# Gathers in a four-layer graph network: what GpSimd waits for before it issues the next one

## What is computed

```python
# layer 0, twice: attention over the incoming edges of a node, 4 heads of 32
kj = k[src] + e
vj = v[src] + e
alpha = einsum('ehc,ehc->eh', q[dst], kj) / sqrt(C)
p = exp(alpha - segment_max(alpha, dst)[dst])
w = p / segment_sum(p, dst)[dst]
out = segment_sum(vj * w, dst) + x @ Ws + bs
# layer 1: an MLP of each node over [x, sum of edge_attr]
# layer 2: relation attention, whose score of an edge has a part from its source
score = s_node[src, etype] + d_node[dst, etype] + s_rel[etype]
# layer 3, twice: a weighted sum of rows of x[src] @ W[edge_type]
out = segment_sum((xj @ W[r]) * edge_weight, dst) + x @ root + bias
```

## Time and profile before

| | us |
|---|---|
| median of 3 runs | 8819.53 |
| lowest, highest | 8816.77, 8831.27 |
| the profiled execution's own time | 8871.76 |
| its span, first to last instruction | 8869.8 |
| busy: PE, DVE, ACT, POOL | 3145.1, 3340.3, 1098.0, 4141.1 |
| mean granted clock of PE | 0.61 of full speed |

### The profile page before, as it was taken

How to read it: one execution, slowest core, us unless ns; L and a number is a source line. 1 busy time by engine, 2 the same in 40 slices (tenths; PEclk the granted TensorE clock), 3 DMA queues, 4 the chain that set the end, 5 groups by cost and what they waited for, 6 DMA issues and landing times. The chain is left out here.

```text
span 8869.8 us, 97993 instructions
## 1 busy us (share of the span) xinstructions
PE 3145.1 (35%) x21507; PEld 2692.6 (30%) x21508; DVE 3340.3 (38%) x8392; ACT 1098.0 (12%) x2790; POOL 4141.1 (47%) x4444
## 2 busy tenths in 40 slices
PE   3455555544444544434420000133222224222222
PEld 1454554542444444423320000122222223222222
DVE  6454444455444444455210002982222222222223
ACT  1222222211222222231000000010000001000000
POOL 1444445432555555512555554124555553555554
PEclk7677776776665555566555555556665567655655
DMA  3444444432333333311210000002111112111111
GB/s 117 120 124 119 125 125 117 126 116 89 90 91 92 92 91 88 92 51 49 71 33 0 0 0 4 0 21 71 38 39 39 39 39 84 38 39 39 39 38 45
DMA packets 396582, 583.18 MB, mean 66 GB/s; under 512 B 112981, under 2 KB 272994, under 8 KB 395874
## 3 DMA queue, kind: packets, MB, share of 16 engines
q0 software_dynamic: 160752, 337.32, 14.0%
q1 hardware_dynamic: 235634, 244.06, 8.5%
HBM read 522.34 MB, written 58.72 MB: 66 GB/s over the span
## 5 line engine op out<-in xcount | busy, mean ns | idle before, releaser
L617 POOL DMA_INDIRECT kv<-kv_table,idx x1760 | 1690.1, 960 | 1769.5 <-DMA kv<-kv_table,idx 1206.1
L1822 POOL DMA_INDIRECT rows_in<-rel_table,idx x1568 | 1489.1, 950 | 1156.0 <-DMA rows_in<-rel_table,idx 585.3
L1116 PE MATMUL ps_s<-rows_in,onehot 128*128 x3520 | 717.5, 387 | 2000.7 <-SPq L1835 1755.0
L1116 PEld LDWEIGHTS ps_s<-rows_in,onehot 128*128 128x128 f32 x3520 | 668.1, 291 | 2050.1 <-issue 2047.8
L1543 POOL DMA_INDIRECT from_src<-score_table,idx x784 | 752.3, 960 | 558.8 <-DMA from_src<-score_table,idx 309.7
L1143 DVE TENSOR_TENSOR acc<-acc,ps_s 128x128 f32 x880 | 250.6, 285 | 1812.0 <-PE ps_s L1116 1779.9
L749 PE MATMUL ps_q<-qsplit,st 128*128 x5280 | 557.9, 290 | 1055.7 <-DVE kv L812 917.6
L735 PE MATMUL ps_s<-pv,lent 128*128 128x136 f32 x3520 | 820.9, 386 | 108.1 <-DVE acc L794 96.4
L812 DVE TENSOR_TENSOR kv<-ps_q,kv 128x528 f32<-128x528 f32 x440 | 303.2, 706 | 1435.2 <-DMA kv<-kv_table,idx 1236.1
L749 PEld LDWEIGHTS ps_q<-qsplit,st 128*128 128x128 bf16 x5280 | 504.1, 133 | 1111.6 <-issue 1097.1
L735 PEld LDWEIGHTS ps_s<-pv,lent 128*128 128x128 f32 x3520 | 706.7, 280 | 149.2 <-DVE acc L794 125.5
(11 more groups left out here) (296 smaller groups left out, 3982.0 us busy)
## 6 DMA issues: line engine op xcount, KB each, us to landing
dl_row<-dloc_slots SPq DMA_DIRECT2D x132, 640.0 KB
eb<-in_edge_attr SPq DMA_DIRECT2D x440, 128.0 KB
kv<-kv_table,idx POOLq DMA_INDIRECT x1760
rows_in<-rel_table,idx POOLq DMA_INDIRECT x1568
flags<-flag_rows SPq DMA_DIRECT2D x88, 168.0 KB
rel_table<-y_out SPq DMA_DIRECT2D x14, 1024.0 KB, 4.3
from_src<-score_table,idx POOLq DMA_INDIRECT x784
rel_table<-y_out SPq DMA_DIRECT2D x14, 768.0 KB, 3.6
```

Of the source, the lines that this page charges most:

```text
L617: pool.indirect_dma_start(kv4[:, k, s, 0:KVW], None, kv_table, bass.IndirectOffsetOnAxis(ap=idx[:, k * CB + s:k * CB + s + 1], axis=0))\
L1116: last_mm = pe.matmul(to, one(n, j), ring_rows(places[m], j), start=(j == 0), stop=(j == 1))
L1822: pool.indirect_dma_start(rows3[:, t, :], None, table, bass.IndirectOffsetOnAxis(ap=idx[:, t:t + 1], axis=0)).then_inc(landed[lane].sem, 16)
```

## The change

The lanes are gone. `indirect_dma_start` gets a second semaphore, `engine_sem=described.sem`, which goes up by one when GpSimd has written the gather's descriptors. Before each gather POOL waits for that count, that is for the end of the issuing work of the gather directly ahead, and no longer for any landing. Landings are counted in a semaphore for each half of the buffer (`gathered[k]`) or each part, and the readers wait on that one. SP fetches the indices of chunk c+2 when the gathers of chunk c have landed, where it waited until DVE had summed chunk c. The order of the instructions on the engines is the same, but that in POOL's loops a register instruction that computes the value to wait for stands ahead of each gather, where it stood ahead of each two. All else is untouched.

```diff
-LANES = 2
@@ conv_stream
-                landed = [signal(f"cs_landed{n}") for n in range(LANES)]
-                TURNS = CB // LANES
+                described = signal("cs_described")
...
                             for s in range(CB):
-                                turn, lane = divmod(s, LANES)
-                                if again or c * CB + s >= LANES:
-                                    pool.wait_ge(landed[lane].sem, landed[lane].at(c * (16 * TURNS) + 16 * turn))
+                                if again or c * CB + s > 0:
+                                    pool.wait_ge(described.sem, described.at(c * CB + s))
                                     pool.sem_inc(issuing.sem, 1)
                                 pool.indirect_dma_start(
                                     kv4[:, k, s, 0:KVW], None, kv_table,
-                                    bass.IndirectOffsetOnAxis(ap=idx[:, k * CB + s:k * CB + s + 1], axis=0))\
-                                    .then_inc(landed[lane].sem, 16)
+                                    bass.IndirectOffsetOnAxis(ap=idx[:, k * CB + s:k * CB + s + 1], axis=0),
+                                    engine_sem=described.sem)\
+                                    .then_inc(gathered[k].sem, 16)
...
                             if later(c, 2):
-                                sp.wait_ge(summed.sem, summed.at(c + 1))
+                                sp.wait_ge(gathered[k].sem, gathered[k].at((j + 1) * (16 * CB)))
                                 sp.sem_inc(issuing.sem, 1)
                                 fetch_idx(c + 2, k)
...
-                            for sig in landed:
-                                dve.wait_ge(sig.sem, sig.at((c + 1) * (16 * TURNS)))
+                            dve.wait_ge(gathered[k].sem, gathered[k].at((j + 1) * (16 * CB)))
@@ relation_scores
-                                    turn, lane = divmod(s, LANES)
-                                    if again or s >= LANES:
-                                        pool.wait_ge(landed[lane].sem, landed[lane].at(i * (32 * TURNS) + 16 * turn))
+                                    if again or s > 0:
+                                        pool.wait_ge(described.sem, described.at(i * (2 * CT) + s))
                                         pool.sem_inc(issuing.sem, 1)
...
-                                for sig in landed:
-                                    act_e.wait_ge(sig.sem, sig.at(i * (32 * TURNS) + (k + 1) * (16 * TURNS)))
+                                act_e.wait_ge(gathered[k].sem, gathered[k].at((i + 1) * (16 * CT)))
@@ rgcn_sums
-                                    turn, lane = divmod(t, LANES)
-                                    if again or t >= LANES:
-                                        pool.wait_ge(landed[lane].sem, landed[lane].at(i * (16 * TURNS) + 16 * turn))
+                                    if again or t > 0:
+                                        pool.wait_ge(described.sem, described.at(i * (2 * RP) + t))
                                         pool.sem_inc(issuing.sem, 1)
...
-                                for sig in landed:
-                                    sp.wait_ge(sig.sem, sig.at(i * (16 * TURNS) + (c + 1) * (16 * OF_PART)))
+                                sp.wait_ge(gathered[c].sem, gathered[c].at((i + 1) * (16 * 2 * RC)))
```

More of the change, by code:

```diff
@@ L565, in conv_stream @@
                 issuing = signal("issuing")
-                idx_in, e_in = ((signal("cs_" + n + "0"), signal("cs_" + n + "1")) for n in ("idx_in", "e_in"))
-                landed = [signal(f"cs_landed{n}") for n in range(LANES)]
-                TURNS = CB // LANES
+                idx_in, gathered, e_in = ((signal("cs_" + n + "0"), signal("cs_" + n + "1")) for n in ("idx_in", "gathered", "e_in"))
+                described = signal("cs_described")
                 kv4 = kv[:, :].rearrange("p (k s c) -> p k s c", k=2, s=CB)
@@ L894, in conv_stream @@
                           cs_stepped=CP * NCH, cs_added=CP * NCH, cs_rescaled=2 * (NCH - 1), cs_chained=LINKS * NCH,
-                          cs_cleared=1, cs_idx_in0=16 * NPAIR, cs_idx_in1=16 * NPAIR,
-                          **{f"cs_landed{n}": 16 * TURNS * NCH for n in range(LANES)})
+                          cs_cleared=1, cs_idx_in0=16 * NPAIR, cs_idx_in1=16 * NPAIR, cs_gathered0=16 * CB * NPAIR,
+                          cs_gathered1=16 * CB * NPAIR, cs_described=CB * NCH)
                 if with_edges:
@@ L1516, in relation_scores @@
                 st_made = (signal("rs_st0"), signal("rs_st1"))
-                issuing = signal("issuing")
+                issuing, described = signal("issuing"), signal("rs_described")
                 kept = (signal("rs_kept0"), signal("rs_kept1"))
-                dl_in, summed = ((signal(n + "0"), signal(n + "1")) for n in ("rs_dl_in", "rs_summed"))
-                landed = [signal(f"rs_landed{n}") for n in range(LANES)]
-                TURNS = CT // LANES
+                gathered, dl_in, summed = ((signal(n + "0"), signal(n + "1")) for n in ("rs_gathered", "rs_dl_in", "rs_summed"))
                 st4 = st[:, :].rearrange("p (k s e) -> p k s e", k=2, s=CB)
@@ L1544, in once @@
                                         from_src[:, s:s + 1], None, flat_scores,
-                                        bass.IndirectOffsetOnAxis(ap=idx[:, s:s + 1], axis=0)).then_inc(landed[lane].sem, 16)
+                                        bass.IndirectOffsetOnAxis(ap=idx[:, s:s + 1], axis=0),
+                                        engine_sem=described.sem).then_inc(gathered[k].sem, 16)
                         once(0, False)
@@ L1797, in rgcn_sums @@
                 idx_ready, issuing, pairs_in, stepped = (signal(n) for n in ("rg_idx", "issuing", "rg_pairs_in", "rg_stepped"))
-                landed = [signal(f"rg_landed{n}") for n in range(LANES)]
-                TURNS = 2 * RP // LANES
-                OF_PART = 2 * RC // LANES
+                gathered = [signal(f"rg_gathered{c}") for c in range(RP // RC)]
+                described = signal("rg_described")
                 rows3 = rows_in[:, :].rearrange("p (t c) -> p t c", c=D)
@@ L1823, in once_round @@
                                         rows3[:, t, :], None, table,
-                                        bass.IndirectOffsetOnAxis(ap=idx[:, t:t + 1], axis=0)).then_inc(landed[lane].sem, 16)
+                                        bass.IndirectOffsetOnAxis(ap=idx[:, t:t + 1], axis=0),
+                                        engine_sem=described.sem).then_inc(gathered[c].sem, 16)
                         once_round(0, False)
@@ L1837, in rgcn_sums @@
                           (lambda place, j: rows_in[:, bass.ds(place * (2 * D) + j * D, D)], pairs_in, stepped, place_of))
-                stage_end(rg_idx=LAPS * (RP // RC), rg_pairs_in=LAPS * RP, rg_stepped=NCH * CP,
-                          **{f"rg_landed{n}": 16 * TURNS * LAPS for n in range(LANES)})
+                stage_end(rg_idx=LAPS * (RP // RC), rg_pairs_in=LAPS * RP, rg_described=2 * RP * LAPS, rg_stepped=NCH * CP,
+                          **{f"rg_gathered{c}": 16 * 2 * RC * LAPS for c in range(RP // RC)})
         tables()
```

## The result

The changed kernel takes 8897.9 us (median of 4 runs, 8893.34 to 8898.57), the kernel before 8820.78 beside it: a ratio of 1.0084, 95% interval [1.0067, 1.0102]. It is slower, by 0.8%, where faster was forecast. Its profiled execution took 8897.98 us with a span of 8896.0; against the profiled execution of before (8871.76) that is only 26 us more. The 8871.76 lies outside the four timed runs of the kernel before (8816.77 to 8831.27).

The account below looks back on a forecast made before the run. The prediction took POOL's issue of indirect gathers to bound the kernel. Stage changes of -36 us and -4 for index copies made -40, so 8819.5 - 40 = 8780 us, range 8690 to 9030.

Parts of the forecast that it names:

- What bounds the kernel: In all five gather stages, 83% of the span, POOL's issue of gathers from start to start sets the time.
- Step (a): Before every gather: the wait for the predecessor's descriptors makes each pause 0.82 us, within bounds of 0.30 and 1.14.
- tail: Rival, all 4112 gathers: the engine's semaphore comes after the bar's end; 0.05 us later gives 8985 us; chance 0.12.
- rows 7: Profile rows of POOL with index copy, wait for that copy, then gather: pauses of 0.84, 0.83 and 0.81 us.
- Step (b): Pauses by stage: convolutions -145 and -105 us, scores +84, aggregations +65 each, sum -36; index copies -4; total -40.
- I put the difference on the median: Baseline: profiled execution 52 us over the runs' median; the -40 was applied to 8819.5, giving 8780 us.
- Step (c): Convolutions: the gain passes through, chunk periods falling 3.3 and 2.4 us, with some 10 us of DVE's cover left.
- Step (d): Elsewhere (SP's index fetches, readers' single counts, POOL's register instruction): extra losses and gains are nothing.
- Step (e): DMA queues: with one start each 1.77 us about two gathers are in flight, as before, so little changes.
- The waits' name: In the profile, POOL's waits before gathers would be put down to POOL itself and not to a DMA.
- Landing waits go and nothing comes in: Rival: POOL's 2101.1 us of landing idle vanishes, leaving 6718 us, or about 6660 by 0.30 us pauses; chance 0.05.
- convolutions without gain: Rival, both convolutions: transfers set the pace, so the -250 stays away and +214 comes, 9030 us; chance 0.08.

Follow-up runs that it names:

- group 2: Changed kernel with no wait between gathers: 9687.84 us; changed kernel with each gather waiting for descriptors of the gather two ahead: 9566.29 us.
- threes: Changed kernel, with POOL waiting for descriptors only before every third gather in all three loops: 8482.16 us, ratio 0.9621.
- pairs: Changed kernel, with POOL waiting for descriptors only before every second gather in all three loops: 7923.47 us, ratio 0.8927.

## Why the prediction was wrong

*What bounds the kernel* held: where the start-to-start time fell and the others were not held back, the stage gained it in full.

*Step (a)* held in mechanism: hardly a pause under 0.8, no tail, a median of 0.81 where I took 0.82. What failed is "every pause becomes that of rows 7". 77 gathers have a pause of over 1.0 us that is no index copy's doing (18 in the convolutions, 7 in the scores, 52 in the aggregations), like the 1.66 at 6215.94, and behind the 123 index copies within the stages it is mostly 0.96 to 0.98 us and not 0.83. Of the 77, 64 stand at fixed places: 3.25 us at every hundredth gather of a convolution, 3.52 at every 112th of the scores, 1.66 (three times 1.98) at every 32nd of an aggregation. They are no landings: at 6215.94 the wait had been met at 6214.32. The 77 cost about 96 us over 0.81, the index copies about 20, and all other pauses, being 0.81 and not 0.82, give back about 51. In the kernel before, the trace shows such a pause at some of these places and not at others, so its waits for landings covered them in part; nothing covers them now. *Step (b)* thereby: pauses 7 and 9 us over the forecast in the convolutions, 10 in the scores, 17 and 17 in the aggregations, together 60; the index copies gained nothing in the changed kernel (idle 16.6 and 16.1 us where 7.8 and 16.6 stood before): +8 and not -4; busy time 9 less. -40 + 60 + 12 - 9 = +23, for a difference of +26 between the two profiled executions. This alone turned the sign: on one chip the change costs 23 us where the sum said -40.

*"I put the difference on the median"* is the second failure, and made a loss of 0.3% one of 0.8%. The profiled execution of before stood 52 us over its median, and I took this for something the change would carry along. The changed kernel has no such gap: profiled 8897.98, median 8897.9. 66 us of the sum and 52 of the baseline are the 118 between 8780 and 8898. The repeated runs speak against the profiler as the cause (8869.1 profiled, 8870.03 timed on one chip) and show that the kernel before differs from one set of runs to the next, each on another chip. It waits for single landings, the changed kernel doesn't, and that one agrees within 5 us in the two sets that timed it. That landings differ by chip is therefore my reading, and shown by no run; why the profiled execution of before stood 52 us apart stays open.

*Step (c)* held: the convolutions are 139 and 100 us shorter for a forecast of 145 and 105, and DVE kept its wait for rows (1005.5 us). *Step (d)* held: the five stages account for 23 of the 26 us. *Step (e)* held: in the convolutions a gather takes some 2.8 us from its start to its landing, with a start each 1.75 us, so one or two are in flight.

*The waits' name* was foretold wrongly: the profile says DMA, not POOL.

*Rivals.* There is no tail: the wait is met 0.034 us after the bar's end, and the pauses are 0.81. The convolutions did gain. "Landing waits go and nothing comes in" got 0.05 and a time of 6660 to 6718 for the case that pauses fall to 0.30. The runs of group 2 made those pauses and took 9688: the price of 0.30, used as bound of (a) as well, had a cost on other engines that no row of before shows. There the Trainium skill, page "DMA: Bandwidth & Descriptors", section "Anatomy of one DMA — SWDGE (gpsimd) path", says that most of such a DMA's fixed time is completion latency. This case's trace agrees (rows land 1.8 us after the bar, median of the convolutions), but the forecast that the rival drew from it fails: 8898 us without waiting for completions, and a larger loss when the pauses are gone.

*The chances*: with 0.01 us of pause worth 41 us, and a median on another footing than the trace, 0.53 for faster was too much for a sum of -40. That 8898 lies within the stated range of 8690 to 9030 bears out nothing: the range was wide for a tail and for convolutions without gain, and neither came.

## What to carry to other kernels

A stream of indirect gathers is paced by what stands between two of them: here 0.30 us with nothing, 0.81 for a wait on the one ahead, about 1.2 for a landing in the convolutions. In this kernel a wait on descriptors before every second or third gather was best. Try the grouping by stage: threes won in the scores and aggregations and lost in the convolutions, where the other queues have more to do. Don't take the shortest pause for the best one without a look at what the other engines do meanwhile. And before a difference of profiles is put on a median, see whether the profiled execution and the timed ones of the kernel before agree.

## What the hardware showed unexpectedly

- With gathers issued at 1.25 us from start to start, the queues of TensorE and SP are held back: the `ps_d` matmuls of a stage take 1406 instead of 391 us, ten DMA issues 21.33 instead of 5.65. At 1.43 and 1.38 us the convolutions still lose hundreds of us. At about 1.5 us little of it is seen (305.2 us of idle time at `ps_d` with pairs against 217.4), or none (215.1 in the kernel with the multiply).
- With a multiply of 0.54 us on POOL between gathers the kernel is 1540 us faster than with a copy of 0.20 us in its place (7736.93 and 9277.11, each on its own chip, where the kernel before takes 8798.5 and 8905.1).
- From POOL's wait on its own work to the next gather 0.81 us pass, behind an independent instruction 0.16.
- A wait for a gather's descriptors is met 0.034 us after its bar ends; the rest of the 0.81 us lies between the met wait and the engine's start.
- The kernel before differs by 1.2% between sets of runs, each on another chip (8798.5 to 8905.1 us).
